# Two-layer graph network on one Trainium2 core: the last MLP's first layer in three fp32r passes and later, two DMAs of the head swapped, a cleared tile for the dummy matmuls, one piece of x in two

## What is computed

```
conv(x, eps, W, b):  h = a@x + (1 + eps) * (a@x);  3 times h = relu(h @ W[i].T + b[i])
m   = concat(conv(x, eps1, W1, b1), conv(x2, eps2, W2, b2)) @ Wm.T + bm
x   = layernorm(x + m)
deg = rowsum(adj + I);  d = rsqrt(deg)
x   = layernorm(x + (d * (adj + I) * d) @ x @ W.T + b)
```

## Time and profile before

| what | us |
|---|---|
| median of 3 runs | 591.78 (591.65 to 592.2) |
| the profiled execution | 591.9 |
| its span, first to last instruction | 590.1 |
| TensorE busy | 582.8 |
| VectorE busy | 545.2 |
| ScalarE busy | 378.4 |

### The profile page before, as it was taken

One profiled execution on the slowest core, in us unless ns is written; L12 is line 12 of the kernel. 1 busy time (PEld: TensorE's weight loads), 2 busy tenths in 40 slices (PEclk: granted clock), 3 DMA queues, 4 the chain that ended last, 5 costly groups with the idle time before them and its releaser, 6 DMA issues.

```text
span 590.1 us, 7652 instructions
## 1 busy us (share of the span) xinstructions
PE 582.8 (99%) x2676; PEld 485.5 (82%) x2676; DVE 545.2 (92%) x692; ACT 378.4 (64%) x510; POOL 28.1 (5%) x26
## 2 busy tenths in 40 slices
PE   8999999999999999999999999999999999999996
PEld 7788888888888888888888888878888888888885
DVE  6999999998987999898799999997999997989986
ACT  6644537852454773353667336479799799799794
POOL 0000000001100000110000020000200001010011
PEclk9999999999999999999999999999999999999998
DMA  8978565443555454354534365675899998999921
GB/s 329 366 279 288 211 219 209 144 148 143 197 190 193 170 175 148 139 193 178 201 142 148 143 259 187 269 305 203 312 364 396 424 382 337 382 351 353 387 82 72
DMA packets 30731, 141.91 MB, mean 240 GB/s; under 512 B 5488, under 2 KB 6256, under 8 KB 16496
## 3 DMA queue, kind: packets, MB, share of 16 engines
q1 hardware_dynamic: 30128, 139.87, 63.7%
q10 hardware_dynamic: 576, 1.70, 0.7%
HBM read 139.40 MB, written 2.16 MB: 240 GB/s over the span
## 4 chain that ended last, share of the span: by engine, by line
PE 92%; DVE 4%; ACT 1%; DMA 1%; issue 1%; SPq 0%; POOLq 0%; POOL 0%; DVEq 0%
PE ps L532 78%; PE pd L553 6%; PE ps L608 6%; PE pd L562 2%; DVE alo L916 1%; PE pd L594 1%; DMA raw<-early 1%; DVE rowsum L927 1%; DVE rowsum L931 0%; ACT outn L752 0%; DVE x1lo L900 0%; DVE x2s L900 0%; ACT ahi L719 0%; DVE z L1212 0%; ACT ahi_extra L719 0%
## 5 line engine op out<-in xcount | busy, mean ns | idle before, releaser
L719 ACT ACTIVATE ahi<-raw 128x1024 fp32r<-128x1024 f32 x212 | 222.3, 1060 | 159.9 <-PE ps L532 154.0
L916 DVE TENSOR_TENSOR alo<-raw,ahi 128x1024 fp32r<-128x1024 f32 x212 | 256.9, 1220 | 27.0 <-ACT ahi L719 26.0
L532 PE MATMUL ps<-ahi,x2s 128*128 128x512 f32 x512 | 138.3, 389 | 0.0
L532 PE MATMUL ps<-ahi,x1hi 128*128 128x512 f32 x384 | 121.9, 393 | 0.0
L532 PE MATMUL ps<-alo,x1hi 128*128 128x512 f32 x384 | 120.4, 389 | 0.3 <-DVE alo L916 0.3
L532 PE MATMUL ps<-ahi,x1lo 128*128 128x512 f32 x384 | 120.7, 390 | 0.0
L532 PEld LDWEIGHTS ps<-ahi,x2s 128*128 128x128 f32 x512 | 96.1, 188 | 20.0
L532 PEld LDWEIGHTS ps<-alo,x1hi 128*128 128x128 f32 x384 | 72.0, 188 | 15.7 <-DVE alo L916 0.7
L532 PEld LDWEIGHTS ps<-ahi,x1lo 128*128 128x128 f32 x384 | 72.4, 188 | 15.1
L532 PEld LDWEIGHTS ps<-ahi,x1hi 128*128 128x128 f32 x384 | 71.9, 189 | 14.9 <-issue 0.5
L532 PE MATMUL ps<-alo,x2s 128*128 128x512 f32 x256 | 80.3, 389 | 0.0
(11 more groups left out here) (102 smaller groups left out, 526.0 us busy)
## 6 DMA issues: line engine op xcount, KB each, us to landing
raw<-a_t SPq DMA_DIRECT2D x108, 1024.0 KB, 4.9
raw<-a_t SPq DMA_DIRECT2D x32, 512.0 KB, 8.6
raw<-early SPq DMA_DIRECT2D x7, 512.0 KB, 7.7
xn<-x SPq DMA_DIRECT2D x3, 1024.0 KB, 8.3
out<-outn ACTq DMA_DIRECT2D x3, 512.0 KB, 6.4
par<-params SPq DMA_DIRECT2D x1, 708.0 KB, 12.9
raw<-head SPq DMA_DIRECT2D x2, 256.0 KB, 3.0
xn<-x SPq DMA_DIRECT2D x1, 512.0 KB, 7.4
```

The lines of the kernel that those rows point to most:

```text
L532: mm = pe.matmul(ps[bank + (CH * (q % 2) if layer else 0)][:, :], block_of(w, n), a[c], start=(n == 0 and k == 0), stop=(n == JB - 1 and k ...
L719: act.activation(ring_hi(layer, q, n), raw_tile(layer, n), ACT.Copy).then_inc(hi_ready, 1)
L916: dve.tensor_tensor(ring_lo(layer, q, n), raw_tile(layer, n), as_f32(ring_hi(layer, q, n)), ALU.subtract).then_inc(lo_ready, 1)
```

## The change

- The first layer of the last MLP becomes three fp32r passes like the others. Its h is rounded by ScalarE behind tiles 3 and 4 and subtracted by VectorE there, two blocks each.
- On TensorE the last MLP's layers stand behind tiles 4, 6, 8 instead of 1, 3, 5, merge behind 10 instead of 6. ScalarE's relus stand behind 7, 9, 10 instead of 4, 6, 7. VectorE's subtractions of h stand in pairs behind 3, 4, 5, 6, 8, 9 instead of in fours behind 4 and 6. What is counted from merge on VectorE (residual, statistics, aggregate, shifts) moves by 4 steps, and so do the scales of y and the steps of y (constants 24 for 20, 27 for 23); the last norms begin at 32 instead of 29.
- SP issues x2's first piece behind the second half of tile 0 instead of ahead of it.
- The dummies multiply a tile `blank` that VectorE clears as its first instruction, not `identity`.
- The piece of x and x2 for the second quarter of blocks comes in two halves, taken behind tiles 5 and 8 instead of whole behind 6; the next piece is taken behind 13 instead of 12.

```diff
--- before.py
+++ after.py
@@ -66,16 +66,16 @@
 
 
 
-PE_DENSE = ({3: 0, 5: 1, 8: 2}, {1: 0, 3: 1, 5: 2})
-PE_MERGE = (10, 6)
-DVE_SPLIT_H = {4: 1, 6: 2}
+PE_DENSE = ({3: 0, 5: 1, 8: 2}, {4: 0, 6: 1, 8: 2})
+PE_MERGE = (10, 10)
+DVE_SPLIT_H = {3: (0, 0), 4: (0, 2), 5: (1, 0), 6: (1, 2), 8: (2, 0), 9: (2, 2)}
 PE_PROJECT = 1
 PE_WARM = 8
 
 
 AHEAD_OF_PE = (SPLIT, SPLIT2)
 ACT_EVACUATE = (2, 2)
-ACT_RELU = ({k + SPLIT: l for k, l in PE_DENSE[0].items()}, {4: 0, 6: 1, 7: 2})
+ACT_RELU = ({k + SPLIT: l for k, l in PE_DENSE[0].items()}, {7: 0, 9: 1, 10: 2})
 DVE_RESIDUAL = (PE_MERGE[0] + SPLIT, PE_MERGE[1] + SPLIT)
 STATISTICS = (2, 2)
 TB = 32
@@ -83,14 +83,14 @@
 DVE_AGGREGATE = tuple(k + 1 + KB // s for k, s in zip(DVE_RESIDUAL, STATISTICS))
 DVE_DEGREES = (DVE_RESIDUAL[0] + 1, 13)
 DVE_FACTORS = (DVE_AGGREGATE[0] + 2, 16)
-ACT_NORM_LAST = 29
+ACT_NORM_LAST = 32
 DVE_TURN = (5, 2)
 DVE_BASE = 10
 DVE_BASE_LAST = 20
 DVE_SHIFT = tuple(k + 2 for k in DVE_AGGREGATE)
-ACT_NORM = (22, 20)
+ACT_NORM = (22, 24)
 ACT_COPY_AY = 3
-DVE_MAKE_Y = (KB + 4, 2 * KB + 4, 3 * KB + 3, 23)
+DVE_MAKE_Y = (KB + 4, 2 * KB + 4, 3 * KB + 3, 27)
 NORM_BLOCKS = (2, 2)
 ACT_ROUND_Y = tuple(k + 1 for k in DVE_MAKE_Y)
 DVE_SPLIT_Y = tuple(k + 2 for k in DVE_MAKE_Y)
@@ -106,7 +106,7 @@
 
 
 
-X_PIECES = [(0, 0, 2), (0, 2, 4), (0, 4, KB), (1, 0, KB), (2, 0, KB), (3, 0, KB)]
+X_PIECES = [(0, 0, 2), (0, 2, 4), (0, 4, KB), (1, 0, HB), (1, HB, KB), (2, 0, KB), (3, 0, KB)]
 X_PIECE_AT = {KB * q + k: i for i, (q, k, _) in enumerate(X_PIECES)}
 
 X_PIECE_START = [2 * P * P * sum(k1 - k0 for _, k0, k1 in X_PIECES[:i]) for i in range(len(X_PIECES))]
@@ -117,7 +117,7 @@
 WOVEN = 3 * KB
 FIRST_ENDS = JB + KB - 1
 SLOT1 = (4, 5, 0, 1, 6, 2, 3, 7)
-X_AFTER = {1: 1, 3: 2, 6: 3, 12: 4, 20: 5}
+X_AFTER = {1: 1, 3: 2, 5: 3, 8: 4, 13: 5, 20: 6}
 
 
 def build(nc, a_t, head, early, x12, params, scratch, out):
@@ -160,6 +160,7 @@
         whi = sb("whi", [P, WM_AT], F32R)
         wlo = sb("wlo", [P, WM_AT], F32R)
         identity = sb("identity", [P, P])
+        blank = sb("blank", [P, P])
         par = sb("par", [P, PARAMS])
         partial = sb("partial", [P, QW // TB])
         regrouped = sb("regrouped", [P, GROUPS, QW // TB])
@@ -252,6 +253,7 @@
         const_step = sem("const_step")
         const_ready = sem("const_ready")
         warm_ready = sem("warm_ready")
+        blank_ready = sem("blank_ready")
         gain_ready = sem("gain_ready")
         whi_ready = sem("whi_ready")
         wlo_ready = sem("wlo_ready")
@@ -366,7 +368,7 @@
                 if q == 2:
                     sp.wait_ge(x_split, 2 * 3)
                 if q == 3:
-                    sp.wait_ge(x_split, 2 * 4)
+                    sp.wait_ge(x_split, 2 * 5)
                 place = 2 * (q % 2)
                 sp.dma_start(xn[:, place:place + 2, k0 * P:k1 * P], x_piece(i)).then_inc(x_in[i], 16)
 
@@ -374,7 +376,7 @@
             _, k0, k1 = X_PIECES[0]
             for c in range(CH):
                 sp.dma_start(raw[:, 0, 0, c * CW:(c + 1) * CW], head[c]).then_inc(half_in[c], 16)
-                if c == 0:
+                if c == CH - 1:
                     sp.dma_start(xn[:, 1, k0 * P:k1 * P], x_piece(0)[1]).then_inc(x2_in, 16)
             sp.dma_start(raw[:, 0, 1], early[0]).then_inc(raw_in[0], 16)
             load_x(1)
@@ -383,6 +385,8 @@
                 sp.dma_start(raw[:, p, 1], early[2 * p]).then_inc(raw_in[p], 16)
                 if p in (1, 3):
                     load_x(2 + p // 2)
+                if p == 3:
+                    load_x(4)
             sp.dma_start(par[:, :], params).then_inc(params_in, 16)
 
             def load(dst, p):
@@ -427,7 +431,7 @@
             for g in (1, 2):
                 for s in range(RAW):
                     load0(g, s)
-                load_x(3 + g)
+                load_x(4 + g)
             for s in range(RAW):
                 load0(3, s)
             with sp.Fori(1, QUARTERS - 1) as q:
@@ -542,12 +546,9 @@
                     if plan == 0:
                         wait(pe, hlo_ready, q * (LAYERS * M) + (M * l + m + 1))
                         passes = ((whi, hhi), (whi, hlo), (wlo, hhi))
-                    elif l:
-                        wait(pe, hlo_ready, q * (LAYERS * M) + (M * (l - 1) + m + 1))
+                    else:
+                        wait(pe, hlo_ready, q * (LAYERS * M) + (M * l + m + 1))
                         passes = ((whi, hhi), (whi, h_rest), (wlo, hhi))
-                    else:
-                        wait(pe, h_ready, q * (4 * M) + (M * l + m + 1))
-                        passes = ((par, h),)
                     at = (W1_AT, W2_AT)[m // CH] + l * P
                     for k, (w, a) in enumerate(passes):
                         mm = pe.matmul(pd[:, m, :], w[:, at:at + P], a[:, m, :], start=(k == 0),
@@ -655,9 +656,9 @@
                     if n == PE_PROJECT:
                         project(before)
 
-            pe.wait_ge(warm_ready, 1)
+            pe.wait_ge(blank_ready, 1)
             for k in range(PE_WARM):
-                pe.matmul(pd[:, 3, 0:P], identity[:, :], identity[:, :], start=True, stop=True)
+                pe.matmul(pd[:, 3, 0:P], blank[:, :], blank[:, :], start=True, stop=True)
             layer0_quarter(0, None)
             pe.wait_ge(const_ready, 2 + GROUPS)
             pe.wait_ge(params_in, 16)
@@ -757,9 +758,9 @@
             def mlp_step(q, n, plan):
                 if n == ACT_EVACUATE[plan]:
                     evacuate(q)
-                if plan == 0 and n in (ACT_EVACUATE[0] + 1, ACT_EVACUATE[0] + 2):
+                if n in (ACT_EVACUATE[plan] + 1, ACT_EVACUATE[plan] + 2):
                     for m in range(CH):
-                        round_h(q, 0, CH * (n - ACT_EVACUATE[0] - 1) + m)
+                        round_h(q, 0, CH * (n - ACT_EVACUATE[plan] - 1) + m)
                 if n in ACT_RELU[plan]:
                     relu(q, ACT_RELU[plan][n], plan)
                 at, size = ACT_NORM[plan], NORM_BLOCKS[plan]
@@ -934,7 +935,7 @@
 
                 if plan == 1:
                     wait(dve, h_ready, q * (4 * M) + (M * l + m + 1))
-                wait(dve, hhi_ready, q * (LAYERS * M) + (M * (l - plan) + m + 1))
+                wait(dve, hhi_ready, q * (LAYERS * M) + (M * l + m + 1))
                 dve.tensor_tensor((hlo, h_rest)[plan][:, m, :], h[:, m, :], as_f32(hhi[:, m, :]),
                                   ALU.subtract).then_inc(hlo_ready, 1)
 
@@ -1152,8 +1153,9 @@
                         mlp_step(LAST, p, 1)
                         y_step(p, (LAST,))
                         if p in DVE_SPLIT_H:
-                            for m in range(M):
-                                split_h(LAST, DVE_SPLIT_H[p], m, 1)
+                            l, first = DVE_SPLIT_H[p]
+                            for m in range(first, first + CH):
+                                split_h(LAST, l, m, 1)
                     finish_step(0, p - FIRST_ENDS - 1)
                     if p == DVE_SECOND_BASE[2]:
                         second_base(2)
@@ -1175,6 +1177,7 @@
                     elif (n + AHEAD2) // KB == q:
                         add_identity(q, n + AHEAD2)
 
+            dve.memset(blank[:, :], 0.0).then_inc(blank_ready, 1)
             _, k0, k1 = X_PIECES[0]
             dve.wait_ge(x_in[0], 16)
             dve.tensor_scalar(x1hi[:, 0, k0 * P:k1 * P], xn[:, 0, k0 * P:k1 * P], 1.0, None,
```

## The result

The change makes the kernel slower: 593.70 us as the median of 13 runs (593.06 to 595.22) against 592.20 for the kernel before in the same stretch of runs; the ratio is 1.0027 with an interval of [1.0019, 1.0035]. The forecast was 592.7, "no difference that can be told". It missed by 1.0 us: 0.4 of this is the median of before, which stood at 591.78 when the forecast was made, and 0.6 is the change itself, 1.5 us slower instead of 0.9. What was measured is a small slowdown that is clear of the noise. The profiled executions say the same: 593.88 against 591.9, and in their spans 592.1 against 590.1.

A forecast was written before the change was run, and what follows sets the result against it. The prediction took VectorE to set the time until 27.05 us and TensorE afterwards, the tail apart. From the profiled 591.9, start -0.6, fp32r layer -0.7 and waits +2.3 gave 592.9, or 592.7 against the median; range 591.4 to 593.7.

The forecast's parts named there:

- the 18.9 I had asked for: Start: the time by about which the half of x must have landed; otherwise 0.4 us is lost.
- The three waits: Last MLP: TensorE waits for VectorE's low parts of tiles 3, 4 and 6, by 0.9, 1.0 and 0.4 us.
- What follows: Steps behind merge in the last MLP: moving them costs 0, bounds 0 and 0.5 us.
- the backlog reaches further: Rival at y_shift and layer 0's relu: VectorE's lateness costs 0.3 to 1.3 us more, total 593.0 to 594.0; chance 0.20.
- the 14.1: Limit for y_shift behind merge's end; each us beyond it costs one at tile 30.
- the 399.5: Limit for the start of ScalarE's layer 0 relu; each us later costs one at tile 6.
- VectorE decides: Start: TensorE leaves tile 7 0.6 us earlier, with a head start of 0.5 as with 0.1.
- The wait of up to 0.5 at tile 6's low part: Start: with a head start of 0.5, TensorE's weight load there waits up to 0.5 us for VectorE.

The follow-up runs named there:

- experiment 11: Kernel before with merge and all that follows, degrees and factors included, 4 tiles later, MLP as before: 592.54 us against 591.97.
- experiment 3: Kernel before with merge and what is counted from it 4 tiles later, degrees left at tile 13, MLP as before: 592.02 us against 592.01.
- Experiment 6: Kernel after with VectorE's degrees at step 10, in its idle time, instead of 13: 593.13 us against 592.27 for the kernel before.
- experiment 5: Kernel after with the row sums' transpose behind tile 3 and their addition behind tile 7: 592.49 us against 592.27 for the kernel before.
- experiment 9: Kernel after with its MLP put back early, dense layers behind 2, 4, 6 and merge behind 7: 592.95 us against 592.18 for the kernel before.
- experiments 8: Kernel before with only x of the second quarter in halves: 592.05 us in a single run, kernel before 592.27.
- 10: Kernel before with only the cleared dummy tile and the swapped DMAs, x whole: 592.04 us against 592.18.
- 7: Kernel after with transpose behind tile 3, addition behind tile 7 and degrees at step 11: 592.79 us against 592.27 for the kernel before.

## Why the prediction was wrong

**What fitted.** The dummies at 1.05 (forecast 1.0). The half of x was rounded at 19.05, hardly later than the 18.9 I had asked for, and tile 7 had no wait. The layer in fp32r: 2.73 instead of 3.43, from the dense rows at 398.01 to the tile behind them at 400.74; forecast -0.71. The three waits: the steps between TensorE's rows give 0.89, 0.98 and 0.41; forecast 0.9, 1.0 and 0.4. Their sum less the layer is +1.6 (the prediction writes +1.5 in one place, but its own terms give 1.6, and its last sum uses them), and merge against T0 moves by 7.04, which is four tiles (5.44) and 1.60. y_shift was ready 14.04 behind merge's end (432.39 against 418.35; forecast 13.97), and tile 30's low part had no wait. Each of these was a sum over rows, and each of the MLP's held within 0.1. The real work at the start came at 4.61, not 4.45.

**The step that failed** is "What follows": "Tile 30 then fits with 0.1 to spare. Taken at 0, bounds 0 and 0.5." This term, the cost of all that stands behind merge, measured 0.9. I had asked whether one tile's low part meets TensorE's due time, and stopped there. But VectorE is without a gap from y's split to first z, and first z is followed by the end at 126.4 to 126.5 in every run of the table. In the kernel before both engines were just in step: TensorE had no wait on a low part of 0.3 us or more behind T0, and VectorE no gap beside it; a VectorE that was 0.39 later cost 0.4 (experiment 11). From the runs the size of it follows:

- first z moves by (shift of y's split) - 1.135 x (tiles moved): after, 7.00 - 4.54 = 2.46; measured 2.46 (76.35 - 73.89).
- With y's split as far behind merge as before (27.71 against 27.75), this is TensorE's 1.60 and 4 x (1.36 - 1.135) = 0.90. VectorE catches up 0.23 with each tile, and a step that is moved by 4 tiles of TensorE's time leaves it 4 tiles fewer to do so.
- That 0.90 could have been paid for: with the degrees ahead of the residual the way from merge to y's split is 0.8 shorter (experiment 3). In the kernel after it is given away again by the residual, 0.92 later behind merge, since four tiles and the degrees stand between the idle time of 2.03 and the residual, three tiles before. Experiment 6 gets it back, and what is then left, 1.53, is TensorE's own loss (1.6).

TensorE's shift, read at its first projection, and VectorE's, read at first z, give the end by the larger of the two: experiment 6 has 1.62 and 1.47 (end 1.53), experiment 5 has 0.60 and 1.18 (end 1.17), experiment 9 has 0.94 and 1.24 (end 1.23), experiment 11 has -0.05 and 0.39 (end 0.44). Only experiment 6 has TensorE's the larger, and by little. I gave "the backlog reaches further" 0.20 and named y_shift and tile 6 as its places. Its price came true (593.0 to 594.0), its places did not: y_shift stayed within the 14.1, and ScalarE's relu began at 398.90, which is 399.35 by the T0 of before and thus ahead of the 399.5, after 1.83 us of waiting for TensorE. That its price fitted is luck.

**The start.** Forecast -0.6; the run with the start alone shows -0.7, at the upper bound of 0.7. "VectorE decides" is only half of it: experiments 8 and 10 show VectorE late without the halves, and TensorE's first operands late in the one execution with the halves alone. The wait of up to 0.5 at tile 6's low part is there in the start alone (0.43), but hardly in the kernel after (0.1), where tile 7 is sooner than before only because tile 1 landed sooner (6.63 against 7.30); the whole start's 0.7 counted from tile 1 shows in five other executions. T0 averages 389.43 over the eight kernels with the whole start (388.75 to 390.15) and 390.27 over the four that have the start of before, a difference of 0.84; the spread is as large, so the size rests on the timed runs, and the gain counted from tile 1 supports its cause. The profile of before, T0 at 389.78, was the best of those four, and so the profile after shows only 0.45. The sum of both, -0.84 and +2.46, is 1.6, or 1.8 with the 0.7 of the timed runs; the medians differ by 1.5.

Whether TensorE's saving could be had in full stays open: no run has both its waits and the residual's delay gone.

## What to carry to other kernels

When an engine reads 99% busy and waits for nothing, another can still be exactly in step with it, as VectorE was here: look in the windows view for a stretch where a second engine is also full, and ask what a delay at the head of that stretch does at its end. A step that is moved later by n tiles is not neutral for an engine that is faster per tile than the bound: it loses n times the difference in catching up (here 4 x 0.225). And put small steps into a gap of the engine that has one, but first look where their data comes from.

## What was unexpected

**Landings at the start vary from execution to execution.** ScalarE's first rounding of tile 1, which waits for the second half MB, came at 7.30 before, at 6.63 after and at 8.47 in experiment 3:

```profile
6.63 1.15 ACT L697 ACTIVATE ahi<-raw 128x512 fp32r<-128x512 f32 x2 [1.05 <-DMA raw<-early]
```

```profile
8.47 1.15 ACT L696 ACTIVATE ahi<-raw 128x512 fp32r<-128x512 f32 x2 [1.97 <-DMA raw<-early]
```

From there to T0 all fourteen profiled executions took 381.9 to 383.1 us, so that a late landing moves the whole kernel. The six without the whole start lie within 382.46 to 382.53; five of the eight with it at 381.93 to 381.97, 0.5 less.

**The clock's rise isn't tied to the work.** Experiments 6 and 7 differ only in the last quarter. The dummies begin at 1.05 in both, and TensorE works on from there, with a pause of at most 0.5 us. In 6 the step between two matmuls of 512 columns is down to 0.23 (2.4 GHz) by 5.63; in 7 it is still 0.41 to 0.43 (1.2 GHz) up to 7.04:

```profile
5.63 0.39 PE L536 MATMUL ps<-ahi,x1lo 128*128 128x512 f32 x1
5.86 0.39 PE L536 MATMUL ps<-alo,x1hi 128*128 128x512 f32 x1
```

```profile
6.63 0.57 PE L536 MATMUL ps<-alo,x1hi 128*128 128x512 f32 x1
7.04 0.62 PE L536 MATMUL ps<-ahi,x2s 128*128 128x512 f32 x2
```

The Trainium skill, TensorE: Matmul & The Clock Gate, section "What's actually happening", says that the activity window runs freely and does not reset with the kernel; the two runs agree with it, being 1.4 us or more apart with the same work ahead.
